# Graph network, layer 2: ScalarE fetches one more 128-row subtile of every four groups row by row

## The chip, the cores and the metric

The kernel runs on one core of a Trainium2 chip. The metric is the device time of one execution in microseconds (us). The core has five engines that work side by side, each with its own instruction stream: PE (matrix multiplications), DVE (elementwise work on tensors), ACT (ScalarE, one function per element), POOL (GpSimd; here it only issues gathers) and SP (SyncE; here it only issues transfers). An engine waits for another by a semaphore that the other counts up.

## The reference

Two message-passing layers run over one graph of 6250 nodes and 200000 edges. Both begin with a normalisation of the node features and a ReLU, and each adds its result to `x`. Layer 1 is an attention over the edges that end at a node. Layer 2, the one that the change touches, maps the node features, reads the row of each edge's source node, weighs it by a small network over the edge's features, and sums over the edges of each target node:

```python
s = s @ W_up_s * inv
v = jnp.einsum('nui,uw->nwi', v, W_up_v) * inv
h = jax.nn.silu(edge_feats @ A1 + b1)
h = jax.nn.silu(h @ A2 + b2)
w0, w1, w2, w3 = jnp.split(h @ A3, 4, axis=1)
ss, vs = s[sender], v[sender]
y_s, y_v = edge_attrs[:, :1], edge_attrs[:, 1:4]
out_s0 = ss * y_s * w0
out_s3 = jnp.einsum('eui,ei->eu', vs, y_v) / R3 * w3
out_v1 = ss[:, :, None] * y_v[:, None, :] * w1[:, :, None]
out_v2 = vs * y_s[:, :, None] * w2[:, :, None]
mji = jnp.concatenate([out_s0, out_s3, out_v1.reshape(E, 3 * MUL), out_v2.reshape(E, 3 * MUL)], axis=1)
message = jax.ops.segment_sum(mji, receiver, num_segments=num_nodes) / 10.0
```

The summed messages of a node are mapped once more by `W_out_s` and `W_out_v`.

## The kernel before

The edges are sorted by target. They are cut into tiles of 1024 edges, a tile into 8 subtiles of 128 (one edge per partition), and four tiles make a group. The place of a tile in its group is its slot s, 0 to 3. There are 49 groups; the code runs them in pairs by `groups` (L307), 24 turns of a loop with an even (e = 0) and an odd group (e = 1), and then one short group alone.

In layer 2 the engines share the work of a tile as follows.

- POOL gathers the source rows of 128 edges with one indirect transfer out of the table `up_tab` (L485), so 8 gathers for a tile. Before the gathers of a tile it waits until PE has summed the tile three places back, whose buffer it fills.
- SP spares POOL one gather in every two groups. The eighth subtile of slot 3 of the odd group is fetched by `fetch_single` (L396 to L402): 128 transfers of one row each, 80 of them during the even group and 48 during the odd one, in lots of 16 with one load of 16 row numbers into registers (L398). They land in one column of the row buffer, `single`. Per group SP then stores the finished node block (L438), loads the edge features (L415) once PE has used the old ones, and loads the edge attributes `y` (L411) once DVE has made the last message of the group (`msg1` of slot 3). All this stands in one queue, so the rows of the next group begin after that last wait.
- ACT runs the two Silu functions of the network for the tile two places ahead (`hidden`, L628 and L630). In slot 2 it also takes part in finishing a node block (`stage_block`): three copies, L635, L638 and L641, with two matrix products of PE between them (`map_block`, L1368 and L1372).
- PE makes, tile by tile and in this order: the radial weights of the next tile (L1358), the first product of the network for the tile two ahead (L1348), the sums of the first half tile (L1401), the second product of the network (L1352), the sums of the second half tile.
- DVE makes the messages of a tile in two halves of four subtiles, L1155 to L1167 each. The first of these instructions waits for the gathered rows. Then come the one-hot matrix of the next tile (L1086), the first weighing of the next tile (L1099), in slot 3 a copy of `y` (L1183), and the addition of the sums of the tile before (L1107). In slot 2 DVE ends with `add_block` (L1080), which adds the finished node block to `x` and waits for ACT's last copy.

No order is planned: each engine runs through its own code in the order written, and the semaphores set the rest.

Of the kernel before, what the change touches and what calls it, by code (L numbers as in the profile page):

```python
# [6 lines left out]
I32 = mybir.dt.int32  # L7
U8 = mybir.dt.uint8
BF16 = mybir.dt.bfloat16
ALU = mybir.AluOpType  # L10
# [32 lines left out]
FIRST = 80  # L43
ERP = 6 * HEADS
# [11 lines left out]
assert 0 < LT < HT and GI % 2 == 1 and QUADS <= 64 and AHEAD == 2 and U == 4  # L56
# [11 lines left out]
def gnn_kernel(nc, x, src, src_single, dst, dst_lin, edge_y, edge_f, bias, front, weights, out):  # L68

    with ExitStack() as ctx:  # L70
# [68 lines left out]
        early = sb("early", [P, max(NG * T, GI // 2 * P)])  # L139
        dst_rel = early[:, 0:NG * T].rearrange("p (g t) -> p g t", t=T)  # L140
        single_i = early[0:1, 0:GI // 2 * P].bitcast(I32)
        win_f = sb("win_f", [P, NG])
# [19 lines left out]
        w_aug = sb("w_aug", [P, LW])  # L162
        ones_row = sb("ones_row", [P, ZW])
        rows_all = sb("rows", [P, U * T + 1, ZW])
        rows = rows_all[:, 0:U * T, :].rearrange("p (u t) f -> p u t f", t=T)
        moved_on = rows_all[:, (U - 1) * T + 1:U * T + 1, :]
        single = rows_all[:, U * T, :]
# [30 lines left out]
        elr = part(3000, NB, 2 * HEADS)  # L198
        bound = part(3784, NB, HEADS)
# [72 lines left out]
        s_l2 = named("l2", ("h1", "h2", "tp", "first", "weighted", "dotted", "single")) | slot_sems("l2", ("h1_act", "h2_act")) \  # L272
# [41 lines left out]
        ROWS_IN = {"rows0": [GI * 16 * HT] * (U - 1) + [(GI - 1) * 16 * HT + 16 * LT],  # L314
                   "rows1": [GI * 16 * HT] * (U - 1) + [(GI - 1) * 16 * HT - GI // 2 * 16]}
# [3 lines left out]
        def slot_rows(s, fetched):  # L319

            return moved_on if fetched and s == U - 1 else rows[:, s, :, :]
# [22 lines left out]
        def _(sp):  # L344
# [61 lines left out]
            sp.dma_start(single_i, src_single).then_inc(loads["single"], 16)  # L406
# [67 lines left out]
        @block.gpsimd  # L474
        def _(pool):

            pool.memset(w_aug[:], 0.0).then_inc(zeroed, 1)
            pool.memset(ones_row[:], 0.0).then_inc(zeroed, 1)
# [4 lines left out]
            def gather(to, indices, table, width, done, n=T):  # L483
                for t in range(n):
                    pool.indirect_dma_start(out=to[:, t, 0:width], out_offset=None, in_=table,  # L485
                                            in_offset=bass.IndirectOffsetOnAxis(ap=indices[:, t:t + 1], axis=0))\
                        .then_inc(done[t // HT], 16)

            pool.wait_ge(G["flags_ready"], 1)
            general = pool.value_load(flags_i[0:1, 1:2], min_val=0, max_val=1)  # L490
            passes1 = pool.value_load(flags_i[0:1, 2:3], min_val=1, max_val=PASSES1)

            pool.wait_ge(s_in["stored_early"], 16 * REUSED)
            pool.wait_ge(s_in["stored"], 16 * (BI - REUSED))
            with pool.If(general > 0):
                with pool.Fori(0, NG) as g:
                    hold(pool, s_max["idx"], g + 1)
                    gather(rows[:, 0, :, :], idx_max, z_tab, ZW, (s_max["rows"],) * 2)
                hold(pool, s_max["free"], NG + 1)

            def gather_edges(tab, width, before, rows_stored):
                with pool.Fori(0, passes1) as k:
                    done = before + k
                    pool.sem_inc(s_l1["open"], 1)
                    if rows_stored:
                        pool.wait_ge(s_mid["stored"], rows_stored)

                    def four_tiles(q, r, e):
                        n = pool.snap(done * GI + q + 1, min_val=1, max_val=2 * PASSES1 * GI)
                        hold(pool, idx_set, done * SETS + q + 1)  # L510
                        for s in range(U):
                            hold(pool, s_l1["agg"][(s - 3) % U], n)
                            short, fetched = isinstance(r, int) and s == U - 1, e == 1 and s == U - 1
                            gather(slot_rows(s, fetched), idx[:, e, s, :], tab, width,
                                   (s_l1["rows0"][s], s_l1["rows1"][s]), LT if short else T - 1 if fetched else T)

                    groups(pool, four_tiles)
                    for half in ("rows0", "rows1"):
                        for s in range(U):
                            hold(pool, s_l1[half][s], ROWS_IN[half][s])  # L520
                    hold(pool, s_l1["msg1"][U - 1], (done + 1) * GI)
                    for half in ("rows0", "rows1"):
                        pool.inc_swdge_sem(s_l1[half], ROWS_IN[half], mode="sub")

            gather_edges(z_tab, ZW, 0, 0)
            gather_edges(up_tab, HIDDEN, passes1, 16 * NB)


        @block.scalar
        def _(act):  # L530
# [59 lines left out]

            with act.Fori(0, passes1) as k:
# [50 lines left out]

            last_stage = last_from(act)
            with act.Fori(0, passes1) as k:
# [7 lines left out]
                def four_tiles(q, r, e):  # L652
# [15 lines left out]
                groups(act, four_tiles)  # L668
# [9 lines left out]
        def _(dve):  # L678
# [85 lines left out]
            def node_rows(s, width):  # L764

                for first, last in ((0, SLOTS), (SLOTS, BI)):
                    if first > 0:
                        dve.wait_ge(s["stored_early"], 16 * REUSED)
                    with dve.Fori(first, last) as q:
# [4 lines left out]
                        for b in range(3):  # L774
# [4 lines left out]
                            if s is s_in:  # L779
                                v.tensor_copy(elr[:, bass.ds(q * BU + 3 * b, m), :], lin[:, :, MW:LW])  # L780
                                ins = v.tensor_tensor(to, lin[:, :, 0:width], bc(ones_row[:, :], 1, m), ALU.add)
# [212 lines left out]
            with dve.Fori(0, passes1) as k:  # L994
# [8 lines left out]
                def four_tiles(q, r, e):  # L1003
# [12 lines left out]
                    for s in range(U):  # L1016
                        h = s % 2
                        ts = slice(0, LT if last and s == U - 1 else T)
                        rows_s = slot_rows(s, e == 1)
                        el_e = rows_s[:, ts, MW:ZW]  # L1020

                        if last and s == U - 1:
                            dve.wait_ge(s_l1["rows0"][s], ROWS_IN["rows0"][s])
# [86 lines left out]
            with dve.Fori(0, passes1) as k:  # L1110
# [8 lines left out]
                def four_tiles(q, r, e):  # L1119
# [5 lines left out]
                    if not isinstance(r, int):  # L1125
                        landed_3 = dve.snap(landed_beside(r, e), min_val=16, max_val=GI * 16 * HT)
# [8 lines left out]
                    for s in range(U):  # L1135
                        h = s % 2
                        short = isinstance(r, int) and s == U - 1
                        for hf in range(1 if short else 2):
                            half = "rows0" if hf == 0 else "rows1"
                            dve.wait_ge(s_l1[half][s], ROWS_IN[half][s] if short else  # L1140
                                        landed_3 if s == U - 1 and hf == 1 else landed)
                            if e == 1 and s == U - 1 and hf == 1:
                                dve.wait_ge(s_l2["single"], fetched)
                            rows_s = slot_rows(s, e == 1)
# [48 lines left out]
                groups(dve, four_tiles)  # L1193
# [13 lines left out]
        def _(pe):  # L1207
# [27 lines left out]
            node_lin(s_in, w_aug[:, :], LW)  # L1235
# [10 lines left out]
            with pe.If(general > 0):  # L1246
                with pe.Fori(0, NG) as g:
                    pe.wait_ge(s_max["rows"], g * (16 * T) + 16 * T)
                    pe.wait_ge(s_max["free"], g + 1)
                    for i in range(T):  # L1250
                        mm = t.transpose(bank[i // 4][0:HEADS, (i % 4) * P:(i % 4) * P + P],
                                         rows[:, 0, i, MW:ZW], ident[:, :])
# [261 lines left out]
```

## Time and profile before

| | us |
|---|---|
| median of 3 runs | 3960.19 (3960.07 to 3960.31) |
| profiled execution | 3959.96 |
| its span in the trace | 3958.1 |
| PE, DVE, POOL busy in the span | 2594.4, 2490.1, 2913.5 |
| ACT busy in the span | 1006.3 |

The profiled execution lies within the runs. Layer 2 fills the time from 2020 us to the end. Register work, branches and the issue of transfers by SP and ACT are not counted as busy, so a busy share says little about SP, and on ACT it tells nothing of time spent on issuing.

### The profile page before, as it was taken

The page shows a single profiled execution, that of the slowest core. Times are in us where ns is not written, and L with a number is a line of the kernel's source. Part 1 is how long each engine was busy: PE and PEld are TensorE (multiplying, and loading weights), DVE is VectorE, ACT ScalarE, POOL GpSimd, SP SyncE. Part 2 cuts the span into 40 slices and gives each one's busy share as a digit, 9 for nine tenths or more (in the row PEclk, how much of TensorE's full clock was granted, in tenths as well). Part 3 has the DMA queues.
Part 4 walks back from the last instruction along what each step waited for, and adds up shares of the span by engine and source line. Part 5 has one row for each costly group of instructions (what it writes and reads, how often), then busy time and mean ns, then how long its engine had stood idle before and what let it go on. Part 6 is the DMA issues. An engine that isn't in the chain of part 4 may idle for free.

```text
span 3958.1 us, 64895 instructions
## 1 busy us (share of the span) xinstructions
PE 2594.4 (66%) x11162; PEld 1893.4 (48%) x11163; DVE 2490.1 (63%) x6074; ACT 1006.3 (25%) x1440; POOL 2913.5 (74%) x3088
## 2 busy tenths in 40 slices
PE   3545455545555555555578878787888888888887
PEld 2444444444444444444445555555555555555554
DVE  7444444444444444444467878887888878887787
ACT  4333333333333333333331111111111111111111
POOL 2777777777777777777767777777777777777776
PEclk8666666666666666666679999999999999999999
DMA  4222222222222222222212222222222222222221
GB/s 130 63 63 62 63 62 62 62 62 62 62 62 62 62 63 63 62 61 63 62 50 59 62 59 62 59 62 59 62 61 60 59 62 62 59 59 63 61 60 53
DMA packets 150584, 248.11 MB, mean 63 GB/s; under 512 B 59341, under 2 KB 97335, under 8 KB 150167
## 3 DMA queue, kind: packets, MB, share of 16 engines
q0 software_dynamic: 98496, 214.52, 21.8%
q1 hardware_dynamic: 51642, 30.27, 2.9%
q14 instruction: 297, 2.43, 0.2%
q10 hardware_dynamic: 144, 0.80, 0.1%
q8 instruction: 5, 0.08, 0.0%
HBM read 235.33 MB, written 10.03 MB: 62 GB/s over the span
## 4 chain that ended last, share of the span: by engine, by line
POOL 43%; issue 21%; PE 12%; DVE 8%; DMA 7%; SPq 5%; DVEq 1%; ACT 0%; POOLq 0%; ACTq 0%
POOL rows L485 43%; PE pair L1401 5%; PE pair L1322 5%; SPq L402 4%; DMA rows<-up_tab,idx 4%; DMA rows<-z_tab,idx 3%; DVE share L1044 2%; SPq L398 1%; PE pair L1358 1%; DVE share L1162 1%; DVE share L1158 1%; DVE acc L935 1%; PE pair L1348 1%; DVE share L1156 0%; PE pair L1352 0%
## 5 line engine op out<-in xcount | busy, mean ns | idle before, releaser
L485 POOL DMA_INDIRECT rows<-z_tab,idx x1539 | 1459.9, 949 | 539.9 <-issue 513.4
L485 POOL DMA_INDIRECT rows<-up_tab,idx x1539 | 1452.1, 944 | 487.3 <-issue 445.6
L1322 PE MATMUL pair<-share,acc 128*128 128x136 f32 x3126 | 750.3, 431 | 806.2 <-DVE share L1044 806.2
L1322 PEld LDWEIGHTS pair<-share,acc 128*128 128x128 f32 x3126 | 695.7, 324 | 939.9 <-DVE share L1044 937.9
L1401 PE MATMUL pair<-share,acc 128*128 128x256 f32 x3126 | 795.8, 399 | 295.2 <-DVE share L1167 291.7
L1401 PEld LDWEIGHTS pair<-share,acc 128*128 128x128 f32 x3126 | 574.9, 193 | 664.8 <-DVE share L1167 567.0
L1033 DVE TENSOR_TENSOR share<-rows,share 128x64 f32<-128x64 f32 x196 | 44.4, 226 | 855.6 <-DMA rows<-z_tab,idx 824.3
L1358 PE MATMUL pair<-weights_sb,share 128*128 128x256 f32 x1568 | 390.8, 394 | 30.5 <-ACT acc L641 29.1
L1155 DVE TENSOR_TENSOR share<-rows,pair 128x384 f32<-128x384 f32 x391 | 216.3, 553 | 302.2 <-DMA rows<-up_tab,idx 282.5
L628 ACT ACTIVATE share<-pair,front_sb 128x512 f32<-128x512 f32 x196 | 134.6, 687 | 927.0 <-PE pair L1348 927.0
L1358 PEld LDWEIGHTS pair<-weights_sb,share 128*128 128x128 f32 x1568 | 307.7, 199 | 84.1 <-issue 39.5
L606 ACT ACTIVATE pair<-share 128x64 f32<-128x64 f32 x196 | 44.6, 228 | 1073.0 <-DVE share L1038 1071.6
L630 ACT ACTIVATE share<-pair,front_sb 128x512 f32<-128x512 f32 x196 | 134.7, 687 | 489.4 <-PE pair L1352 487.3
L1044 DVE SCALAR_TENSOR_TENSOR share<-pair,rows 128x1088 f32<-128x1088 f32 x196 | 250.7, 1279 | 0.3 <-ACT pair L606 0.3
L935 DVE TENSOR_TENSOR acc<-acc,pair 128x1024 f32<-128x1024 f32 x196 | 239.1, 1220 | 0.1
L1086 DVE TENSOR_TENSOR acc<-acc,pair 128x1024 f32<-128x1024 f32 x196 | 237.5, 1212 | 0.0
L1162 DVE TENSOR_REDUCE share<-share 128x128 f32<-128x384 f32 x391 | 228.4, 584 | 0.0
L584 ACT ACTIVATE acc<-acc,ones 128x1024 bf16<-128x1024 bf16 x196 | 225.0, 1148 | 6.4
L1348 PE MATMUL pair<-ef_sb,weights_sb 64*128 64x512 f32 x392 | 223.4, 650 | 0.8 <-ACT share L630 0.8
L581 ACT ACTIVATE acc<-pair,acc 128x1024 bf16<-128x1024 f32 x196 | 215.8, 1101 | 25.2 <-PE pair L1265 25.2
L1158 DVE TENSOR_TENSOR share<-rows,pair 128x384 f32<-128x384 f32 x391 | 213.6, 546 | 0.0
L1164 DVE TENSOR_TENSOR share<-share,pair 128x384 f32<-128x384 f32 x391 | 212.1, 542 | 0.0
(168 smaller groups left out, 2384.8 us busy)
## 6 DMA issues: line engine op xcount, KB each, us to landing
rows<-z_tab SPq DMA_DIRECT2D x3072, 0.6 KB
rows<-up_tab SPq DMA_DIRECT2D x3072, 0.5 KB
rows<-z_tab,idx POOLq DMA_INDIRECT x1539
rows<-up_tab,idx POOLq DMA_INDIRECT x1539
ef_sb<-in_edge_f SPq DMA_DIRECT2D x50, 128.0 KB
z_tab<-rows SPq DMA_DIRECT2D x7, 504.0 KB, 3.2
y_sb<-in_edge_y SPq DMA_DIRECT2D x50, 64.0 KB
x_sb<-in_x SPq DMA_DIRECT2D x7, 448.0 KB, 7.0
```

What stands on the lines that cost most here:

```text
L485: pool.indirect_dma_start(out=to[:, t, 0:width], out_offset=None, in_=table, in_offset=bass.IndirectOffsetOnAxis(ap=indices[:, t:t + 1], a ...
L584: nc.scalar.activation(to, to, ACT.Relu, bias=ones[:, 0:1], scale=-2.0).then_inc(s_l1["turned"][s], 1)
L935: v.tensor_tensor(hot[:, s, :, :], bc(dst_col[:, bass.ds(group, 1), :].rearrange("p a t -> p (a t)"), 2, P), bc(iota_l1, 1, T), ALU.is_equal)
L1044: v.scalar_tensor_tensor(out=msg[:, h, ts, :].rearrange("p t (h f) -> p t h f", f=RW), in0=bc(a_ps[h][:, ts, :], 3, RW), scalar=1.0, in1=r ...
L1086: v.tensor_tensor(hot[:, s, :, :], bc(dst_col[:, bass.ds(group, 1), :].rearrange("p a t -> p (a t)"), 2, P), bc(iota_l2, 1, T), ALU.is_equal)
L1155: v.tensor_tensor(vy, vecs, y_v, ALU.mult)
L1158: v.tensor_tensor(cell[:, :, 0:96].rearrange("p t (i u) -> p t i u", u=MUL), vecs, bc(w[:, :, 2 * MUL:3 * MUL], 2, 3), ALU.mult)
L1162: v.tensor_reduce(dots, vy.rearrange("p t i u -> p t u i"), AX.X, ALU.add)\
L1322: mm = t.matmul(bank[2 + h][:, 0:MW], hot[:, s, i, :], msg[:, h, i, :], start=(i == 0), stop=(i == tiles - 1))
L1348: t.matmul(bank[4], a1_bd[at, s, :], ef_sb[at, :], start=True, stop=True).then_inc(s_l2["h1"], 1)
L1358: mm = t.matmul(bank[2 * (s % 2) + j // 2][:, (j % 2) * 256:(j % 2) * 256 + 256], h2_sb[:, s % 2, j * P:(j + 1) * P], a3_bd[:, :], start=T ...
L1401: mm = t.matmul(bank[6 + s % 2][:, 0:MSG], hot[:, s, j, :], msg2[:, s % 2, hf, j % HT, :], start=(j == 0), stop=(j == tiles - 1))
```

## The change

In layer 2, POOL no longer gathers the first subtile of slot 2 in every fourth group (f = 3, with f the place of a group in a loop over four groups). ACT fetches its 128 rows by one-row transfers into a new column of the row buffer, `ahead`. It does so in 13 lots of 12 and 8 rows, one behind the second Silu of each tile from slot 0 of f = 0 to slot 0 of f = 3. In slot 2 the lot stands ahead of ACT's work on the node block. DVE waits for the rows ahead of the first half of that tile, and ACT waits in slot 3 of f = 3 until DVE has used them. The layer-2 loops of POOL, ACT and DVE are now four groups long (`groups4`); those of SP and PE keep their length. Layer 1 keeps its gathers. To make room, two small tensors (`w_aug`, `ones_row`) move into a shared buffer.

```diff
+STEPS = (12, 8) * 6 + (8,)
...
+        rows_all = sb("rows", [P, U * T + 2, ZW])
+        ahead = rows_all[:, 2 * T, :]
+        single = rows_all[:, U * T + 1, :]
...
+        def groups4(eng, body):
+
+            with eng.Fori(0, GI // 4) as w:
+                for f in range(4):
+                    body(w * 4 + f, w * 2 + f // 2, f % 2, w, f)
+            body(GI - 1, GI // 2, 0, GI // 4, 0)
...
-            gather_edges(z_tab, ZW, 0, 0)
-            gather_edges(up_tab, HIDDEN, passes1, 16 * NB)
+                            in_front = f == 3 and s == 2
+                            gather(slot_rows(s, beside or in_front), idx[:, e, s, :], tab, width,
+                                   (s_l1["rows0"][s], s_l1["rows1"][s]), 1 if in_front else 0,
+                                   LT if short else T - 1 if beside else T)
...
+            gather_edges(z_tab, ZW, 0, 0, ROWS0["z"], groups)
+            gather_edges(up_tab, HIDDEN, passes1, 16 * NB, ROWS0["up"], groups4)
...
+            def fetch_ahead(tab, width, w, step, fetched):
+
+                first = sum(STEPS[:step])
+                _, nodes = nc.values_load_multi_w_load_instructions(
+                    ahead_i[0:1, bass.ds(w * P + first, STEPS[step])], engines=(mybir.EngineType.Activation,), min_val=0,
+                    max_val=NODES - 1, skip_runtime_bounds_check_because="they are sources, below NODES")
+                for i, node in enumerate(nodes):
+                    act.dma_start(ahead[first + i:first + i + 1, 0:width], tab[bass.ds(node, 1), 0:width])\
+                       .then_inc(fetched, 16)
...
+                        if not isinstance(r, int) and f * U + s < len(STEPS):
+                            fetch_ahead(up_tab, HIDDEN, w, f * U + s, s_l2["ahead"])
+                        if f == 3 and s == 3:
+                            hold(act, s_l1["msg0"][2], n_2)
                         if s == 2:
                             hold(act, s_l1["added"][0], n)
                             blocks(act, mybir.EngineType.Activation, q + 1, stage_block)
...
-                groups(act, four_tiles)
+                groups4(act, four_tiles)
...
+                            if in_front and hf == 0:
+                                dve.wait_ge(s_l2["ahead"], fetched_2)
...
-                groups(dve, four_tiles)
+                groups4(dve, four_tiles)
```

On POOL, the loop of layer 2 before: two groups to a turn, 32 and 31 gathers (L307 is the loop, L284 a wait).

```order
L307 ISA
L284 ISA
L485 DMA rows<-up_tab,idx 128x128 x32
L284 ISA x2
L485 DMA rows<-up_tab,idx 128x128 x31
L307 REGISTER_ALU
L307 COMPARE_AND_BRANCH
```

The same loop on POOL in the change, where the lines are L316, L286 and L502:

```order
L316 ISA
L286 ISA
L502 DMA rows<-up_tab,idx 128x128 x32
L286 ISA x2
L502 DMA rows<-up_tab,idx 128x128 x31
L286 ISA x2
L502 DMA rows<-up_tab,idx 128x128 x32
L286 ISA x2
L502 DMA rows<-up_tab,idx 128x128 x30
L316 REGISTER_ALU
L316 COMPARE_AND_BRANCH
```

Four groups took two turns with 126 gathers; they now take one with 125.

On ACT, slot 2 of a group before, from the first Silu to the first copy of the node block (L284 is the wait for DVE's addition, L289 and L290 load the numbers of the blocks that are ready):

```order
L627 REGISTER_ALU
L628 ACTIVATE share<-pair,front_sb 128x512
L630 ACTIVATE share<-pair,front_sb 128x512
L284 ISA
L289 TENSOR_LOAD ready
L289 ISA x2
L290 ISA
L290 TENSOR_LOAD ready
L290 ISA x2
L291 COMPARE_AND_BRANCH
L292 UNCONDITIONAL_BRANCH
L292 ISA
```

The same place on ACT in the change, at f = 0 (the Silu lines are L657 and L659, the wait is L286; the pair of L617 rows stands there 12 times, once a row fetched):

```order
L657 ACTIVATE share<-pair,front_sb 128x512
L659 ACTIVATE share<-pair,front_sb 128x512
L613 ISA
L613 TENSOR_LOAD early
L617 ISA
L617 DMA rows<-up_tab 1x128
...
L286 ISA
L291 ISA
L291 TENSOR_LOAD ready
L291 ISA x2
L292 ISA
```

The load of the 12 row numbers and the 12 transfers stand between the second Silu and everything that ACT does for the node block. Counted in the same listing, one turn of the loop of layer 2 has 256 rows on DVE and 67 on ACT before, and 514 and 414 now.

## Rows read from the trace of the kernel before

**Rows 1.** Stretch: length, busy of PE, PEld, DVE, ACT, POOL, granted clock, DMA share, GB/s.

```profile
2100.00:3000.00 900.00, 728.89 (x2696) 485.74 (x2696) 722.83 (x1786) 152.48 (x271) 680.17 (x721) 0.99 0.23 60
```

**Rows 2.** POOL's groups of instructions, 2100 to 3900 us: busy, mean ns, idle before.

```profile
L485 POOL DMA_INDIRECT rows<-up_tab,idx x1442 | 1360.6, 944 | 439.9 <-issue 399.9 <-PE pair L1401 39.9
```

**Rows 3.** Waits of DVE, 2100 to 3900 us: total, times, longest.

```profile
DVE share L1155 <- DMA rows<-up_tab,idx: 268.2, 154, 2.3
DVE x_sb L1080 <- ACT acc L641: 64.5, 43, 2.8
DVE share L1155 <- DMA rows<-up_tab: 5.6, 4, 2.3
```

**Rows 4.** Timeline of DVE: one tile without a wait, start and duration.

```profile
2264.78 0.55 DVE L1155 TENSOR_TENSOR share<-rows,pair 128x384 f32<-128x384 f32 x1
2272.56 0.55 DVE L1155 TENSOR_TENSOR share<-rows,pair 128x384 f32<-128x384 f32 x1
```

**Rows 5.** Timelines of DVE and then ACT: slots 2 and 3 of one group.

```profile
2401.26 0.56 DVE L1155 TENSOR_TENSOR share<-rows,pair 128x384 f32<-128x384 f32 x1
2412.53 0.55 DVE L1155 TENSOR_TENSOR share<-rows,pair 128x384 f32<-128x384 f32 x1
2417.32 0.28 DVE L1167 TENSOR_TENSOR share<-share,pair 128x128 f32<-128x128 f32 x1
2420.49 0.55 DVE L1155 TENSOR_TENSOR share<-rows,pair 128x384 f32<-128x384 f32 x1
...
2406.78 0.69 ACT L630 ACTIVATE share<-pair,front_sb 128x512 f32<-128x512 f32 x1 [2.74 <-PE pair L1352]
2408.34 0.42 ACT L635 ACTIVATE acc<-acc 128x256 f32 x1 [0.87 <-issue]
2410.67 0.38 ACT L638 ACTIVATE acc<-pair 128x256 f32<-128x256 f32 x1 [1.91 <-PE pair L1368]
2411.85 0.28 ACT L641 ACTIVATE acc<-pair 128x128 f32<-128x128 f32 x1 [0.80 <-PE pair L1372]
2415.61 0.69 ACT L628 ACTIVATE share<-pair,front_sb 128x512 f32<-128x512 f32 x1 [3.48 <-PE pair L1348]
```

**Rows 6.** Timeline of PE: the transposes for the node block of that group.

```profile
2410.25 0.38 PE L1368 MATMUL pair<-front_sb,acc 128*128 128x128 f32 x2
```

**Rows 7.** Timeline of SP's transfers: one turn of its loop.

```profile
2658.99 39.44 SPq L402 DMA_DIRECT2D rows<-up_tab  x80
...
2702.36 0.37 SPq L411 DMA_DIRECT2D y_sb<-in_edge_y  x1
2704.02 23.11 SPq L402 DMA_DIRECT2D rows<-up_tab  x48
...
2732.26 0.36 SPq L411 DMA_DIRECT2D y_sb<-in_edge_y  x1
2737.55 2.43 SPq L402 DMA_DIRECT2D rows<-up_tab  x6
```

**Rows 8.** SP's loads of `y` at both ends of another turn, and DVE within it.

```profile
3600.02 0.36 SPq L411 DMA_DIRECT2D y_sb<-in_edge_y  x1
...
3677.35 0.36 SPq L411 DMA_DIRECT2D y_sb<-in_edge_y  x1
...
3674.51 0.56 DVE L1155 TENSOR_TENSOR share<-rows,pair 128x384 f32<-128x384 f32 x1 [2.26 <-DMA rows<-up_tab]
```

**Rows 9.** The page's queue of fetched instructions: packets, MB, share of 16 engines.

```profile
q14 instruction: 297, 2.43, 0.2%
```

**Rows 10.** SP's one-row transfers of layer 2: min, median, max ns.

```profile
L402 SPq DMA_DIRECT2D rows<-up_tab x3072: 237/237/320, 2020.1 to 3909.2; - x192
```

**Rows 11.** Timelines of ACT and SP at the start.

```profile
0.73 0.40 ACTq L543 DMA_DIRECT2D share<-in_dst  x1
...
0.74 0.40 SPq L345 DMA_DIRECT2D front_sb<-in_front  x1
```

**Rows 12.** A stretch behind a pause of PE, columns as in rows 1.

```profile
2217.60:2221.00 3.40, 3.01 (x7) 2.48 (x8) 3.29 (x10) 0.00 (x0) 2.49 (x3) 0.50 0.23 61
```

More of the change, by code:

```diff
@@ L54 @@
 LW = ZW + HEADS
-assert 0 < LT < HT and GI % 2 == 1 and QUADS <= 64 and AHEAD == 2 and U == 4
+assert 0 < LT < HT and GI % 4 == 1 and sum(STEPS) == P and QUADS <= 64 and AHEAD == 2 and U == 4
 assert NB == BU * BI and NG == U * GI and NG * GE >= EDGES and PAD_DST >= NODES + 3 * P and WIN + HALF - 1 <= P
@@ L271, in gnn_kernel @@
                                                          "exp", "msg0", "msg1", "agg", "added", "rows0", "rows1"))
-        s_l2 = named("l2", ("h1", "h2", "tp", "first", "weighted", "dotted", "single")) | slot_sems("l2", ("h1_act", "h2_act")) \
+        s_l2 = named("l2", ("h1", "h2", "tp", "first", "weighted", "dotted", "single", "ahead")) | slot_sems("l2", ("h1_act", "h2_act")) \
             | {n: sems(f"l2_{n}_buf", 2) for n in ("y", "ef")}
@@ L405, in _ @@
             sp.wait_ge(G["columns_set"], 1)
-            sp.dma_start(single_i, src_single).then_inc(loads["single"], 16)
+            sp.dma_start(singles_i, src_single).then_inc(loads["single"], 16)
             sp.wait_ge(s_in["stored_early"], 16 * REUSED)
@@ L481, in _, with gather @@
             pool.memset(minus_id, 0.0).then_inc(zeroed, 1)
-            def gather(to, indices, table, width, done, n=T):
-                for t in range(n):
+            def gather(to, indices, table, width, done, first=0, last=T):
+                for t in range(first, last):
                     pool.indirect_dma_start(out=to[:, t, 0:width], out_offset=None, in_=table,
@@ L497, in _, with gather_edges @@
                     hold(pool, s_max["idx"], g + 1)
-                    gather(rows[:, 0, :, :], idx_max, z_tab, ZW, (s_max["rows"],) * 2)
+                    gather(slot_rows(0), idx_max, z_tab, ZW, (s_max["rows"],) * 2)
                 hold(pool, s_max["free"], NG + 1)
-            def gather_edges(tab, width, before, rows_stored):
+            def gather_edges(tab, width, before, rows_stored, landed0, over):
                 with pool.Fori(0, passes1) as k:
@@ L512, in four_tiles @@
                             hold(pool, s_l1["agg"][(s - 3) % U], n)
[L513 to L518, printed above, removed]
+                            short, beside = isinstance(r, int) and s == U - 1, e == 1 and s == U - 1
+                            in_front = f == 3 and s == 2
+                            gather(slot_rows(s, beside or in_front), idx[:, e, s, :], tab, width,
+                                   (s_l1["rows0"][s], s_l1["rows1"][s]), 1 if in_front else 0,
+                                   LT if short else T - 1 if beside else T)
+                    over(pool, four_tiles)
+                    for half, rows_in in (("rows0", landed0), ("rows1", ROWS1)):
                         for s in range(U):
-                            hold(pool, s_l1[half][s], ROWS_IN[half][s])
+                            hold(pool, s_l1[half][s], rows_in[s])
                     hold(pool, s_l1["msg1"][U - 1], (done + 1) * GI)
-                    for half in ("rows0", "rows1"):
-                        pool.inc_swdge_sem(s_l1[half], ROWS_IN[half], mode="sub")
-            gather_edges(z_tab, ZW, 0, 0)
-            gather_edges(up_tab, HIDDEN, passes1, 16 * NB)
+                    for half, rows_in in (("rows0", landed0), ("rows1", ROWS1)):
+                        pool.inc_swdge_sem(s_l1[half], rows_in, mode="sub")
+            gather_edges(z_tab, ZW, 0, 0, ROWS0["z"], groups)
+            gather_edges(up_tab, HIDDEN, passes1, 16 * NB, ROWS0["up"], groups4)
         @block.scalar
@@ L641, in stage_block @@
                 nc.scalar.activation(moved, mapped_ps, ACT.Copy).then_inc(s_out["moved"], 1)
+            act.wait_ge(loads["single"], 16)
             last_stage = last_from(act)
```

65 lines of the change are left out of this document (40 added, 25 removed).

## The prediction

> **What bounds the kernel now.** I read four views, in this order. First the windows: in layer 2 no engine is busy all the time; in 900 us POOL works 680 us, PE 729, DVE 723 [rows 1]. So I asked who waits. POOL's gathers take 944 ns each, and the idle time in front of them, 439.9 us over 1442 gathers, is mostly put down to "issue", a wait for nothing that the profile shows [rows 2]. One gather therefore costs (1360.6 + 439.9) / 1442 = 1.249 us, back to back. DVE waits 154 times, 268.2 us in all, for POOL's rows, and only 4 times for SP's [rows 3]. POOL sets the pace: two groups have 63 gathers, 63 x 1.249 = 78.7 us, and SP's loop repeats after 2737.55 - 2658.99 = 78.56 us [rows 7].
>
> Two other chains are close behind, and the reader should see how close. DVE needs 2272.56 - 2264.78 = 7.78 us for a tile without a wait [rows 4], 7.96 for slot 3 and 11.27 for slot 2 of this group, which finishes a node block [rows 5] (a wait for late rows lies inside it, but ACT's work on the block ends later anyway). SP's loop is the other. In one turn DVE stood 2.26 us for SP's rows, and SP's load of `y` came 3677.35 - 3600.02 = 77.33 us after that of the turn before [rows 8]. That is what SP needs when nobody delays it: 1.2 us less than POOL.
>
> **What is removed.** Twelve gathers: 12 x 1.249 = 15.0 us, if POOL stays the bound. Four groups then take 125 x 1.249 = 156.1 us instead of 157.3 (measured 2 x 78.56 = 157.1). The other chains must fit into 156.1.
>
> **What is added on ACT.** 128 one-row transfers per four groups. The nearest rows are SP's, with the same instructions: 80 rows take 39.44 us and 48 take 23.11, so (39.44 - 23.11) / 32 = 0.510 us a row, loads of the row numbers included [rows 7]. A lot of 12 costs 6.1 us, one of 8 costs 4.1. The ends: the transfer instruction alone takes 0.237 us [rows 10], so 2.8 us for 12; above 0.510 I have no row, only two queues in each other's way (below). I take 0.510, since it is the same sequence.
>
> In slots 0, 1 and 3 the lot lies beside other work. The second Silu starts 5.52 us into the tile [rows 5], the lot of 12 ends at 11.6, and the next first Silu would be due at 7.78 + 3.08 = 10.9 (3.08 is 2415.61 - 2412.53). It comes 0.7 us late, but the second Silu sat idle 2.74 us before it started [rows 5], which takes that up. Without this cover, each lot of 12 would cost 0.7 us.
>
> In slot 2 nothing covers it when the group finishes a block. Behind the lot on ACT stand the wait for DVE's addition, the loads of the block numbers and the three copies; PE waits for these copies, and DVE waits at L1080 for the last. From DVE's first instruction of slot 2 to that of slot 3 [rows 5]: 5.52 to the second Silu; 6.1 for the lot; 1.56 from that Silu to the first copy; 0.84 to the second copy (0.42 for the first copy, and 0.42 from PE's transposes at 2410.25 [rows 6] to the second copy; today's 2.33 holds a wait for PE's sums, which will be over by then); 1.18 to the third; 0.68 to slot 3. The sum is 15.9 us, against 11.27 today. About every group finishes one block: 43 waits at L1080 in 45 groups [rows 3]. Groups without one give time back and those with two cost more; I let these cancel, plus or minus 10 us on the total.
>
> **What is added at the loop's end.** At a turn of SP's loop, the first row follows the load of `y` after 5.29 us (2737.55 - 2732.26); within a turn the same step takes 1.66 (2704.02 - 2702.36) [rows 7]. So SP pays 3.63 us for a jump back. The queue of fetched instructions moved 297 packets, 2.43 MB [rows 9], so some loop is fetched again at every turn. DVE passes the end of a pair without a wait: 3.17 us from its last message instruction to the next group's first [rows 5], all of it work. Its loop doubles from 256 to 514 listed rows, longer than SP's. The price of the new turn lies between 0, as DVE pays now, and 3.63, as SP pays. I take 2.0, a little above the middle: DVE's engine still has some 3 us of work behind its last message, and how far its instruction stream is ahead of that no row shows. ACT's loop grows as well; its stall lies beside DVE's.
>
> The Trainium skill, "Runtime: NRT & Kernel Launch", section "Instruction fetch mechanics", speaks against the change here: it says that an engine holds 512 instructions in two pages, and that a jump out of them waits for a fetch. The trace agrees that a jump can cost 3.63 us on SP. By this rule DVE would pay the whole of it, and the sum below would be 12 x 1.63 = 20 us higher, about 3992.
>
> **The sum.** Take SP's turns, which end with the last message of an odd group. From the end of f = 3 to that of f = 1, DVE runs back to back: 2.89 to the next group (2420.49 - 2417.60), 2.0 for the jump, 15.56 for two tiles, 15.9, 7.96, 15.56, 15.9, and 5.07 to the last message of slot 3 (2417.60 - 2412.53): 80.8 us. SP cannot begin the rows of f = 2 before that, since its rows stand behind the wait for this message. From there to the end of f = 3, DVE needs 2.89 + 15.56 + 15.9 + 7.96 + 15.56 + 11.27 + 5.07 = 74.2, but SP needs 77.3, and its rows end the wait. Four groups take 80.8 + 77.3 = 158.1 us, against 157.1 before and 156.1 for POOL. That is 1.0 us more in each of 12 turns: 12 us on the profiled execution's 3959.96 (the median of the runs is 0.2 higher), so **3972 us**, 0.3% slower. The gain from POOL is given back twice over: DVE and ACT lose it in the slots with a block, and SP, which can't run ahead of DVE, can't make it up.
>
> Three edits I cost at nothing. DVE's wait for the rows of `ahead`: the last lot is in slot 0 of f = 3, two tiles (15.6 us) ahead; if it were late, its remainder would be paid. ACT's wait in slot 3 of f = 3 for DVE's use of them: DVE has passed that a tile earlier, and behind it stands only the set of indices, which waits for a later message anyway. PE's clock: behind a pause PE was granted 0.50, the lower level of 1.2 GHz, for 3.4 us with 3.01 busy [rows 12], and the lot makes PE pause some 6 us. At full clock this work would take 1.5 us less; DVE needs PE's next weights only at the end of its two halves, some 5 us on, so I count 0; without that cover it is up to 1.5 in each of the two slots, 36 us in all.
>
> **The rivals.** *The gain is kept, POOL stays the bound: 3959.96 - 15.0 = 3945.* It decides once the chain is 2.0 us shorter than my 158.1. One thing suffices: no stall at DVE's jump, or 0.425 instead of 0.510 us a row in the two lots of 12 that are in the way (24 x 0.085 = 2.0). For it: DVE shows no stall at a turn now, and the transfer itself takes 0.237 us. Against it: SP pays both prices in full. Chance 0.30.
>
> *Half of each: no change.* With a stall of 0.5 to 1.5, or rows of 0.45 to 0.49 us, four groups take 156.6 to 157.8, so 3953 to 3968. The rows are fetched by another engine and nothing comes of it. Chance 0.16.
>
> *ACT's and SP's transfers get in each other's way.* During ACT's lots SP issues as many rows. If a row waits while the other engine's 0.237 us [rows 10] run, it finds them with a chance of 0.237 / 0.510 and waits half of them: 0.055 us. For the 48 rows in the half of the turn that SP bounds this is 2.6 us, 12 x 2.6 = 32; the two lots of 12 add 24 x 0.055 = 1.3, another 16: 4004 to 4020. Against it: at the start ACT and SP issued at 0.73 and 0.74 us and both took 0.40 [rows 11], side by side. Chance 0.10. The Trainium skill, "Perfetto Trace Analysis", section "DMA Instruction — HWDGE (DVE, Sync)", has the generator of descriptors locked for exclusive use, which would be this rival; the two rows at the start do not bear it out.
>
> **How the numbers follow.** My forecast has 0.44, with a range of its own of 3962 to 3992 (the blocks' 10 us below, the whole stall above). Of that, 0.10 is for the full stall of 3.63 us at each jump, 3992 (12 x 1.63 = 20 us more). The range for 8 in 10 reaches down to the gain kept, 3943, and up to 4000; it leaves out the contention and a clock that costs its full price. A measurement of this kernel can tell about 0.2%, 8 us, from no change. Faster by more than that: the first rival and a little, 0.31. Within it: the second and the low edge of the forecast, 0.20. Slower: 0.49.
>
> **What would show it.** Right: POOL waits for PE's sums (L1401) by more than 0.3 us, at least from the middle of layer 2, instead of never; the wait at L1080 grows from 1.5 to about 6 us in groups f = 0, 1, 2; a gap of about 2 us at DVE's jump; and in f = 3, DVE waits for SP's rows. Wrong: POOL's gathers still follow each other at 1.249 us to the end (then the chain fits and 3945 holds), ACT's rows under 0.43 us, no gap at the jump, or one-row transfers of more than 0.237 us on SP while ACT fetches.

## The result and the profile after

The changed kernel takes 4037.89 us (median of 4 runs, 4035.47 to 4039.77), against 3960.19 before: a ratio of 1.0196 (95% interval 1.0178 to 1.0214), 78 us slower where 12 were forecast. The time lies outside the range. The profiled execution took 4035.47 us, with a span of 4033.6.

The lost time is all in layer 2. The waits of DVE and of POOL in the changed kernel, from 2100 to 3900 us (total, times, longest), answer to [rows 2, 3]:

```profile
DVE x_sb L1115 <- ACT acc L670: 344.7, 42, 13.1
DVE share L1199 <- issue: 22.6, 11, 2.4
DVE share L1199 <- DMA rows<-up_tab: 20.7, 11, 4.6
DVE share L1199 <- DMA rows<-up_tab,idx: 1.9, 2, 1.3
...
L502 POOL DMA_INDIRECT rows<-up_tab,idx x1378 | 1301.6, 945 | 498.9 <-issue 407.9 <-PE pair L1445 91.0
POOL rows L502 <- PE pair L1445: 91.0, 45, 9.3
```

DVE no longer waits for POOL's rows (1.9 us for 268.2). It waits for ACT's last copy of the node block instead, 8.2 us each time for 1.5 (344.7 / 42; 64.5 / 43 before). POOL waits for PE's sums by up to 9.3 us: the bound has moved from POOL to the chain through DVE, ACT and PE. The same stretch by engine, to be read beside [rows 1], has the granted clock of TensorE as its third number from the end:

```profile
2100.00:3000.00 900.00, 746.10 (x2600) 508.37 (x2601) 690.34 (x1721) 149.12 (x264) 653.34 (x692) 0.88 0.23 59
```

PE finished fewer products in it (2600 for 2696) and was busy longer, at 0.88 of full clock for 0.99. Slot 2 of the group at f = 1 shows where that comes from: the timelines of DVE, ACT and PE, and two stretches of it with the clock.

```profile
3064.56 0.55 DVE L1199 TENSOR_TENSOR share<-rows,pair 128x384 f32<-128x384 f32 x1
3083.20 0.29 DVE L1115 TENSOR_TENSOR x_sb<-x_sb,acc 128x128 f32 x1 [10.92 <-ACT acc L670]
3083.47 0.56 DVE L1199 TENSOR_TENSOR share<-rows,pair 128x384 f32<-128x384 f32 x1
...
3062.62 0.69 ACT L657 ACTIVATE share<-pair,front_sb 128x512 f32<-128x512 f32 x1 [5.42 <-issue]
3065.50 3.27 ACTq L617 DMA_DIRECT2D rows<-up_tab  x8
3071.82 0.69 ACT L659 ACTIVATE share<-pair,front_sb 128x512 f32<-128x512 f32 x1 [2.10 <-PE pair L1396]
3073.02 5.07 ACTq L617 DMA_DIRECT2D rows<-up_tab  x12
3079.89 0.42 ACT L664 ACTIVATE acc<-acc 128x256 f32 x1 [7.38 <-issue]
3081.08 0.38 ACT L667 ACTIVATE acc<-pair 128x256 f32<-128x256 f32 x1 [0.78 <-PE pair L1412]
3082.78 0.28 ACT L670 ACTIVATE acc<-pair 128x128 f32<-128x128 f32 x1 [1.31 <-PE pair L1416]
...
3080.36 0.69 PE L1412 MATMUL pair<-front_sb,acc 128*128 128x128 f32 x2 [6.85 <-ACT acc L664]
3083.46 3.65 PE L1402 MATMUL pair<-weights_sb,share 128*128 128x256 f32 x8 [0.72 <-ACT acc L670]
...
3071.00:3079.00 8.00, 2.50 (x10) 1.52 (x8) 1.26 (x4) 0.69 (x1) 6.17 (x7) 0.85 0.23 60
3079.00:3083.50 4.50, 1.95 (x7) 1.27 (x7) 0.30 (x2) 1.08 (x3) 3.28 (x5) 0.50 0.34 88
```

From DVE's first instruction of slot 2 to that of slot 3 it takes 18.91 us (15.9 were forecast). Term by term, forecast in brackets: 7.26 to the second Silu (5.52), 8.07 from there to the first copy (7.66), 1.19 to the second (0.84), 1.70 to the third (1.18), 0.69 to slot 3 (0.68). The lot itself costs 0.4 us more than was said. But PE, which waits 6.85 us for the first copy, comes back at 0.50 of its clock, the 1.2 GHz level. Its transposes take 0.69 us for 0.38 [rows 6], and the weights for the next tile 3.65 us, where 1.89 is their duration at full clock elsewhere in this trace. Over the groups that finish one block (the first turn left out), slot 2 takes 17.6, 19.3 and 18.8 us on average at f = 0, 1 and 2, and the clock is 0.50 from the first copy to slot 3 in every one of them.

SP's loads of `y` at the ends of the two halves of that turn:

```profile
3003.59 0.36 SPq L428 DMA_DIRECT2D y_sb<-in_edge_y  x1
...
3088.79 0.36 SPq L428 DMA_DIRECT2D y_sb<-in_edge_y  x1
...
3166.36 0.36 SPq L428 DMA_DIRECT2D y_sb<-in_edge_y  x1
```

The first half takes 85.2 us (80.8 forecast), the second 77.6 (77.3). The shape of the sum was right; the error sits in the first half, which holds two of the three blocks with a lot ahead of them; most of what the third loses is hidden behind SP.

### The profile page after: what moved, and what is told of

It is laid out like the page before. It is cut to its first block, busy times and chain, and to the rows that moved or that the text cites. A ratio compares the mean times of both kernels' runs of the same rounds, so it can differ in the third digit from the quotient of the medians.

```text
span 4033.6 us, 69793 instructions
## 1 busy us (share of the span) xinstructions
PE 2674.5 (66%) x11162; PEld 1967.3 (49%) x11163; DVE 2477.2 (61%) x6074; ACT 1009.8 (25%) x1440; POOL 2904.6 (72%) x3076
## 4 chain that ended last, share of the span: by engine, by line
POOL 25%; PE 22%; issue 20%; SPq 12%; DVE 10%; ACTq 6%; DMA 3%; ACT 1%; DVEq 1%; POOLq 0%
POOL rows L502 25%; SPq L419 9%; PE pair L1445 7%; PE pair L1366 4%; PE pair L1402 4%; ACTq L617 4%; DMA rows<-z_tab,idx 3%; PE pair L1392 2%; PE pair L1396 2%; SPq L415 2%; DVE share L1079 2%; PE pair L1416 1%; DVE share L1206 1%; ACTq L613 1%; DVE share L1202 1%
## 5 line engine op out<-in xcount | busy, mean ns | idle before, releaser
L502 POOL DMA_INDIRECT rows<-up_tab,idx x1527 | 1442.3, 945 | 571.2 <-issue 469.2
L502 POOL DMA_INDIRECT rows<-z_tab,idx x1539 | 1460.8, 949 | 539.6 <-issue 513.3
L1366 PEld LDWEIGHTS pair<-share,acc 128*128 128x128 f32 x3126 | 696.1, 324 | 940.5 <-DVE share L1079 938.5
L1445 PEld LDWEIGHTS pair<-share,acc 128*128 128x128 f32 x3126 | 597.3, 196 | 370.7 <-issue 197.1
L1402 PE MATMUL pair<-weights_sb,share 128*128 128x256 f32 x1568 | 445.3, 435 | 30.5 <-ACT acc L670 29.0
L1402 PEld LDWEIGHTS pair<-weights_sb,share 128*128 128x128 f32 x1568 | 340.1, 220 | 97.4 <-issue 42.7
L657 ACT ACTIVATE share<-pair,front_sb 128x512 f32<-128x512 f32 x196 | 134.7, 687 | 753.2 <-PE pair L1392 534.4
L1115 DVE TENSOR_TENSOR x_sb<-x_sb,acc 128x128 f32 x49 | 14.6, 297 | 396.2 <-ACT acc L670 374.9
L1199 DVE TENSOR_TENSOR share<-rows,pair 128x384 f32<-128x384 f32 x391 | 215.8, 552 | 68.3 <-issue 25.3
L659 ACT ACTIVATE share<-pair,front_sb 128x512 f32<-128x512 f32 x196 | 134.7, 687 | 428.8 <-PE pair L1396 428.8
L1392 PE MATMUL pair<-ef_sb,weights_sb 64*128 64x512 f32 x392 | 238.7, 691 | 0.8 <-ACT share L659 0.8
L1396 PE MATMUL pair<-share,weights_sb 128*128 128x512 f32 x392 | 209.1, 616 | 20.2 <-ACT share L657 20.2
```

The lines of the kernel that those rows point to most:

```text
L1366: mm = t.matmul(bank[2 + h][:, 0:MW], hot[:, s, i, :], msg[:, h, i, :], start=(i == 0), stop=(i == tiles - 1))
L1392: t.matmul(bank[4], a1_bd[at, s, :], ef_sb[at, :], start=True, stop=True).then_inc(s_l2["h1"], 1)
L1396: t.matmul(bank[4], a2_bd[:, :], h1_sb, start=True, stop=True).then_inc(s_l2["h2"], 1)
L1402: mm = t.matmul(bank[2 * (s % 2) + j // 2][:, (j % 2) * 256:(j % 2) * 256 + 256], h2_sb[:, s % 2, j * P:(j + 1) * P], a3_bd[:, :], start=T ...
L1445: mm = t.matmul(bank[6 + s % 2][:, 0:MSG], hot[:, s, j, :], msg2[:, s % 2, hf, j % HT, :], start=(j == 0), stop=(j == tiles - 1))
```

## The experiments

Theory A: the lot in front of the block in slot 2 is the loss, by its length and by what the pause does to PE's clock. Rival B: ACT's issuing delays the Silu functions in whatever slot it stands. Rival C: the loops of four groups are too long. Each ratio is to the kernel before on the same chip.

**The lot behind the block.**

```diff
-                        if not isinstance(r, int) and f * U + s < len(STEPS):
-                            fetch_ahead(up_tab, HIDDEN, w, f * U + s, s_l2["ahead"])
                         if f == 3 and s == 3:
                             hold(act, s_l1["msg0"][2], n_2)
                         if s == 2:
                             hold(act, s_l1["added"][0], n)
                             blocks(act, mybir.EngineType.Activation, q + 1, stage_block)
+                        if not isinstance(r, int) and f * U + s < len(STEPS):
+                            fetch_ahead(up_tab, HIDDEN, w, f * U + s, s_l2["ahead"])
```

> The change, with ACT's lot of slot 2 behind its work on the node block instead of ahead of it; the same 13 lots, the same loops. Theory A (the loss sits in slot 2: the lot stands in front of the block's three copies, and the pause that it gives PE lowers PE's clock, which makes the rest of the tile longer): slot 2 of a group with a block falls from 17.3 to 18.9 us back to about 11.5, POOL is the bound again, 3945 to 3952 us. Rival B (ACT's issuing delays the Silu functions wherever the lot stands, and PE and DVE with them): the lot still delays the first Silu of slot 3, over 4000 us. Rival C (the loops of four groups are too long, and their jumps and fetches cost the time): no change from 4038 us.

Measured: 3951.41 us, ratio 0.9963 (0.9949 to 0.9977), 14.5 us less than before. DVE's waits, 2100 to 3900 us:

```profile
DVE share L1199 <- DMA rows<-up_tab,idx: 232.3, 143, 3.0
DVE x_sb L1115 <- ACT acc L670: 66.5, 46, 3.0
DVE share L1199 <- issue: 22.6, 11, 2.3
```

DVE waits for POOL's rows again, and the block costs it 1.4 us a time as before the change. The same 128 rows, on the same engine, in the same loops, now cost nothing, and POOL's gain of 15.0 us arrives. Rivals B and C fall as explanations of the 78 us; B comes back below in a weaker form.

**The loops alone.** POOL gathers everything, ACT fetches nothing, the loops stay four groups long. The counts that POOL and DVE wait for follow, and ACT's wait in slot 3 of f = 3 goes (not shown).

```diff
-                            in_front = f == 3 and s == 2
+                            in_front = False
...
-                        if not isinstance(r, int) and f * U + s < len(STEPS):
-                            fetch_ahead(up_tab, HIDDEN, w, f * U + s, s_l2["ahead"])
```

> The loops of four groups on POOL, DVE and ACT alone: POOL gathers every subtile as before the change, ACT fetches nothing. Theory A: DVE shows a gap of 2.05 us at each of its 12 jumps, as in the changed kernel, but it lies inside the time that DVE waits for POOL's rows anyway: 3958 to 3963 us. Rival C: the 12 jumps and the fetches cost 25 us or more, 3985 us and up. Rival B has nothing to say: 3960 us.

Measured: 3965.44 us, ratio 1.0000 (0.9990 to 1.0009), with 3965.86 for the kernel before on this chip; it is the ratio that answers the expectation. DVE's waits:

```profile
DVE share L1195 <- DMA rows<-up_tab,idx: 252.2, 145, 2.3
DVE share L1195 <- issue: 21.5, 11, 2.1
```

The jump is there, 21.5 / 11 = 1.95 us each, but DVE would have waited for POOL anyway. Rival C is out.

**PE kept busy through the pause.** The clock alone: the lots stay, and PE runs products that nobody reads before it waits for ACT. PE's loop becomes four groups long for it.

```diff
+            def keep_busy():
+                for _ in range(24):
+                    t.matmul(bank[0][:, 0:MSG], ident[:, :], a3_bd[:, :], start=True, stop=True)
...
+                            if f < 3 and not isinstance(r, int):
+                                keep_busy()
                             blocks(pe, mybir.EngineType.PE, q + 1, map_block)
...
-                groups(pe, four_tiles)
+                groups4(pe, four_tiles)
```

> The change, and in addition PE runs 24 products whose result nobody reads, in slot 2 of the groups f = 0, 1, 2, between its sums and its wait for ACT's first copy, where it stood idle for about 7 us (PE's loop is made four groups long for it). It prices the clock alone: the lots stay where they are. Theory A with the clock as a part of it: PE's stages in the block go from 1.19 and 1.69 us (between ACT's copies) to 0.95 and 1.18, the Silu functions come in time again, slot 2 takes 16.3 to 16.6 us in all three groups, and the time is 3985 to 4005 us. If the clock has no part: slot 2 stays at 17.3 to 18.9, 4030 to 4040 us.

Measured: 4078.27 us, ratio 1.0285 (1.0268 to 1.0303). Outside both expectations, and inconclusive: the 24 products took 10.52 us, longer than the pause, and delayed the block themselves. So the same with 14:

> As the run with PE kept busy, with 14 products for 24: the 24 took 10.5 us, 3.2 us longer than the pause that they were to fill, and 14 take 6.1. It prices the clock alone. If the lower clock has a part in the loss: slot 2 with a block takes 16.3 to 16.6 us in f = 0, 1 and 2 (5.52 to the second Silu, 8.2, 0.94, 1.19, 0.68), and the ratio to the kernel before is 1.004 to 1.012. If not: 1.018 to 1.021, as the change.

Measured: 3996.83 us, ratio 1.0091 (1.0074 to 1.0108). Slot 2 of one group at f = 1, DVE and then ACT:

```profile
2412.39 0.55 DVE L1199 TENSOR_TENSOR share<-rows,pair 128x384 f32<-128x384 f32 x1
2428.81 0.56 DVE L1199 TENSOR_TENSOR share<-rows,pair 128x384 f32<-128x384 f32 x1
...
2417.91 0.69 ACT L659 ACTIVATE share<-pair,front_sb 128x512 f32<-128x512 f32 x1 [2.36 <-PE pair L1396]
2425.99 0.42 ACT L664 ACTIVATE acc<-acc 128x256 f32 x1 [7.39 <-issue]
2426.93 0.38 ACT L667 ACTIVATE acc<-pair 128x256 f32<-128x256 f32 x1 [0.53 <-PE pair L1416]
2428.12 0.28 ACT L670 ACTIVATE acc<-pair 128x128 f32<-128x128 f32 x1 [0.80 <-PE pair L1420]
```

16.42 us: 5.52, 8.08, 0.94, 1.19, 0.69. The clock is kept: 0.95 to 1.00 from the first copy to slot 3 in all groups with one block at f = 0, 1 and 2 (the first turn left out), and PE's steps there are short in each. The second Silu comes earlier at f = 1 and 2, after 6.03 and 6.10 us on average for 7.59 and 7.48 in the change, but later at f = 0, after 6.67 for 5.76. So slot 2 kept to the expected 16.6 us in 10 of these 28 groups only; in the others it took 17.0 to 18.8. PE's longer loop is no rival for the gain: PE waits put down to "issue" are 1.4 us in the change and 2.7 here, from 2100 to 3900 us. The work added to PE made the kernel (1.0196 - 1.0091) x 3960 = 42 us faster than the change. That is the clock's part of the 78, less what the products themselves cost, and 36 us remain.

**No rows in slot 2, and what went wrong with that.**

```diff
-STEPS = (12, 8) * 6 + (8,)
+STEPS = (14, 14, 0, 14) * 3 + (2,)
```

> The change with no rows in slot 2: lots of 14 in slots 0, 1 and 3, and 2 in the last one. Theory A2 (the lot in front of the block delays DVE; only when DVE is late and must run at 7.8 us a tile do the lots of the other slots delay the Silu functions too, since at POOL's pace of 9.8 us they fit): slot 2 takes 11.5 us, POOL stays the bound, ratio 0.995 to 0.998. Rival B (a long lot delays the Silu functions in any slot, whatever the pace): the lots of 14 are the longest of all, ratio above 1.01.

Measured: 4023.89 us, ratio 1.0167 (1.0150 to 1.0184), a miss for theory A2. The loads of the row numbers on ACT (L613), minimum, median and maximum in ns, show why: for this kernel, then for one with lots of 12, 12, 0 and 16 rows (below).

```profile
L613 ACTq TENSOR_LOAD <-early x120: 669/1414/3244, 2041.3 to 3949.6; - x120
...
L613 ACTq TENSOR_LOAD <-early x120: 730/967/1068, 2040.7 to 3869.5; - x120
```

Some loads take over 3 us, although they fetch 14 numbers at most. They are those of the lots that begin at row 14, 42, 70 and 98, two past a multiple of four; the lots of 14 from 0, 28, 56, 84 and 112 took 1.2 to 1.4. To test it, each load starts at the multiple of four below and drops the first two numbers; rows, slots and lots are the same.

```diff
-                    ahead_i[0:1, bass.ds(w * P + first, STEPS[step])], ...
+                    ahead_i[0:1, bass.ds(w * P + (first - first % 4), STEPS[step] + first % 4)], ...
-                for i, node in enumerate(nodes):
+                for i, node in enumerate(nodes[first % 4:]):
```

> The run with lots of 14 and none in slot 2, where a load of row numbers that started two past a multiple of four took 3.1 to 3.2 us and one that started at a multiple of four 1.2 to 1.4. Now each load starts at the multiple of four below (16 numbers, of which the first two are not used); rows, places and lots are the same. If the start of the load is the cause: those loads take 1.1 to 1.5 us, and with 2 us less in every second lot the ratio falls from 1.017 to 0.996 to 1.003. If rather 14 rows are too many for the slots (rival B): the loads may be shorter, but the ratio stays over 1.01.

Measured: 3952.59 us, ratio 0.9970 (0.9959 to 0.9982). The loads:

```profile
L613 ACTq TENSOR_LOAD <-early x120: 495/1226/1441, 2043.3 to 3881.1; - x120
```

That settles the miss. It also says what is left of rival B: lots that are some 2 us longer, in slots 0, 1 and 3, do cost time, since they delay the second Silu of slot 2 and the block behind it. With the slow loads it came 11.6 to 14.8 us into slot 2 (means at f = 0 to 2, groups with one block), where the kernel before has 5.7 to 5.8. With the padded ones it is still late, 8.4 to 11.1 us, but this stays hidden: four groups take 156.6 us on average, POOL's pace.

**Four rows, ahead of the block and behind it.** Both have lots of 14, 10, 4 and 10 rows, so both have such slow loads too.

```diff
+STEPS = (14, 10, 4, 10) * 3 + (14,)
```

> The change with lots of 14, 10, 4 and 10 rows in slots 0 to 3 (and 14 in the last one), so slot 2 has 4 rows ahead of the block instead of 12 and the other slots have more. Theory A: the lot of 4 takes about 2.1 us, slot 2 with a block takes some 13.6 us, DVE's group 37 us, under POOL's 39: 3945 to 3955 us. Rival B: the lots of 14 delay the Silu functions more than those of 12, over 4040 us. Rival C: 4038 us.

Measured ahead of the block: 4085.3 us, ratio 1.0321 (1.0261 to 1.0380). That is far above what theory A expected, and is what rival B said.

> The lots of 14, 10, 4 and 10 rows that gave 1.032, with the 4 rows of slot 2 behind the block instead of ahead of it; nothing else differs. Theory A2: those 2.1 us ahead of the block were what set DVE behind POOL, and with them gone everything fits again: 0.995 to 0.998. Rival B: the lots of 14 and 10 were the loss, 1.02 to 1.03.

Measured behind it: 3953.96 us, ratio 0.9986 (0.9976 to 0.9995). This is a little above what theory A2 expected, and rival B is out: the lots and the slow loads (2.2 to 2.5 us for 10 numbers, 3.2 to 3.4 for 14) are the same in both, and the second Silu of slot 2 is late in both, 7.7 to 12.7 us ahead of the block and 8.1 to 10.7 behind it (means at f = 0 to 2). The place of four rows alone is worth 3.3% here. Without the slow loads the same four rows ahead of the block give 1.0031 (next), so the slow loads and these four rows cost far more together (3.2%) than either alone (nothing, and 0.3%).

**The number of rows ahead of the block.** 128 rows in all, every lot at a multiple of four. Slot 2 has 0, 4, 8, 12 (the change) or 16 rows, and the other slots share the rest.

```diff
+STEPS = (12, 12, 0, 16) * 3 + (8,)
...
+STEPS = (12, 12, 4, 12) * 3 + (8,)
...
+STEPS = (8, 12) * 6 + (8,)
...
+STEPS = (8, 8, 16, 8) * 3 + (8,)
```

> No rows in slot 2, lots of 12, 12 and 16 in slots 0, 1 and 3 and 8 in the last: every lot starts at a multiple of four rows, so that no load of row numbers takes 3.2 us, as half of those did in the run with lots of 14. Theory A2 (the lot in front of the block is the loss): ratio 0.995 to 0.999. Rival B (as many rows on ACT cost the same in any slot): 1.015 to 1.02, as with the lots of 14.

> 4 rows in slot 2 ahead of the block, 12 in the three other slots, 8 in the last lot, all from multiples of four rows. Theory A2: the lot ahead of the block takes 2.2 us, slot 2 some 14 us, and DVE's group of 37 to 38 us is still under POOL's 39; with 8 rows the ratio was 1.010 and with 12 it was 1.020, so by that line 0.997 to 1.003. Rival B: about 1.02, since the rows are as many.

> The change with the two sizes swapped: 8 rows in slots 0 and 2, 12 in slots 1 and 3; the lot of slot 2 is still ahead of the block. Theory A2: the lot of 8 takes 4.0 us for 5.5, so slot 2 takes some 15.8 us in f = 0, and DVE still falls behind POOL: ratio 1.005 to 1.015. Rival B: as many rows in all, 1.02. If the lot's place in slot 2 did not matter in proportion to its length: 1.02 as well.

> 16 rows in slot 2 ahead of the block, 8 in all other slots. Theory A2: 1.6 us more ahead of each block than in the change, ratio 1.025 to 1.035. Rival B: the other slots have less, so 1.01 to 1.02.

| rows in slot 2 | median us | ratio to before | 95% interval |
|---|---|---|---|
| 0 | 3945.02 | 0.9961 | 0.9947 to 0.9975 |
| 4 | 3971.97 | 1.0031 | 1.0015 to 1.0048 |
| 8 | 4000.89 | 1.0103 | 1.0086 to 1.0119 |
| 12 | 4037.89 | 1.0196 | 1.0178 to 1.0214 |
| 16 | 4083.24 | 1.0316 | 1.0299 to 1.0333 |

The loss grows with the rows in front of the block, by 0.7% to 1.2% for each four. ACT fetches 128 rows in all five, so the sum of its rows does not explain it, and the other slots have most rows where the loss is least. The stages behind the ratios were longer than theory A2 expected: slot 2 with one block took 14.7, 16.1 and 17.2 us on average at f = 0, 1 and 2 with four rows (some 14 expected), and 16.9 at f = 0 with eight (15.8). With four rows theory A2 expected that DVE would still keep under POOL's pace (0.997 to 1.003); 1.0031 lies just outside, and its ten runs spread from 3957.78 to 3983.88, which fits a point where DVE's chain and POOL are nearly even. In the kernel with none, slot 2 of a group runs nearly as before the change:

```profile
3022.80 0.55 DVE L1199 TENSOR_TENSOR share<-rows,pair 128x384 f32<-128x384 f32 x1
3033.95 0.29 DVE L1115 TENSOR_TENSOR x_sb<-x_sb,acc 128x128 f32 x1 [1.25 <-ACT acc L670]
3034.21 0.55 DVE L1199 TENSOR_TENSOR share<-rows,pair 128x384 f32<-128x384 f32 x1
```

11.41 us, with 11.27 in [rows 5]. At 3945.02 us it is 15.3 us faster than the kernel before on the same chip (3960.29): the whole price of twelve gathers. It is the best version found; the one with the lot behind the block is as good within the intervals.

## Why the prediction was wrong

**Right in its mechanism.** Twelve gathers are worth 15.0 us (15.3 and 14.5 measured, where nothing else was in the way). The lot stands on DVE's path in slot 2, POOL ends up waiting for PE's sums, and DVE waits at its last block instruction, as forecast. The rival in which the gain is kept was worked out to the right time, 3945, but not to the right condition: it takes the lot out of the way of the block.

**The step that failed: "PE's clock ... so I count 0".** The forecast saw that the lot would make PE pause, and priced the lower clock at up to 36 us, but took it for covered: DVE needs PE's next weights only some 5 us on. That looked at one product. The lower clock lies also on the path of the block (1.19 and 1.70 us for 0.94 and 1.18 between ACT's copies) and behind it on PE, whose next products feed the Silu functions that ACT needs before the next lots. The run with 14 products sets the clock's part at 42 us. That this is close to the 36 is luck: the 36 were counted for another path, the weights that DVE waits for.

**The second term that was too small: the second Silu at 5.52 us.** I took the Silu functions as in time in slots 0 and 1, 0.7 us late at worst and covered. In the changed kernel the second Silu of slot 2 came after 5.76 us on average at f = 0, but after 7.59 and 7.48 at f = 1 and 2, and after 7.26 in the group shown. PE's rows ahead of that group, and one of its waits from 2100 to 3900 us, say why:

```profile
3041.00 3.77 PE L1402 MATMUL pair<-weights_sb,share 128*128 128x256 f32 x8 [0.72 <-ACT acc L670]
3044.70 1.70 PE L1392 MATMUL pair<-ef_sb,weights_sb 64*128 64x512 f32 x2
...
3063.36 1.12 PE L1396 MATMUL pair<-share,weights_sb 128*128 128x512 f32 x2 [0.46 <-ACT share L657]
...
PE pair L1396 <- ACT share L657: 15.2, 25, 2.5
```

Behind the block of f = 0, at the lower clock, the weights and the first product take 3.77 and 1.70 us; at full clock they take 1.89 and 1.12. So PE is 2.46 us late. From there to the next block it waits once, 0.46 us, for a first Silu that the lot of 12 in slot 0 held back (the row at 3062.62, idle 5.42, "issue"), and it has not caught up by the second Silu of f = 1. The lots' hold on the first Silu cost PE at most 15.2 us in all of that stretch. The two errors are thus largely one: the clock makes PE late, and PE makes the Silu late. The cover was counted at POOL's pace of some 9.8 us a tile; a DVE that is late runs its tiles at 7.78 [rows 4], and then PE and ACT have too little slack beside it to catch up.

Of the 36 us that remain without the clock's part, 12 were forecast. For the other 24 there is an estimate from the run with 14 products: at f = 0 and 1, slot 2 with one block took 17.73 and 16.93 us on average for 15.9, 2.9 more in the two together. Of these, 1.7 are a second Silu that is still late (6.67 and 6.03 for 5.52) and 1.0 are the way from there to the first copy (8.25 and 8.08 for 7.66). No run separates the two.

**Sized right.** A lot of 12 on ACT: 8.07 us from the second Silu to the first copy, with 7.66 forecast. The jump of DVE's loop: 22.6 / 11 = 2.05 us each, with 2.0 forecast; since that was a choice between 0 and 3.63, it is in part luck. The page's queue of fetched instructions moved 435 packets for 297:

```profile
q14 instruction: 435, 3.56, 0.3%
```

The Trainium skill, "Runtime: NRT & Kernel Launch", section "Instruction fetch mechanics", by which DVE would pay for a jump, holds in kind: the gap appeared with the longer loop, though with 2.05 us and not SP's 3.63. That it costs time does not follow, since in the run with the loops alone it was covered. SP's bound in the second half: 77.6 us for 77.3.

**The contention rival.** It gave 4004 to 4020 and would have been the nearest, for a wrong reason. The one-row transfers of ACT and of SP in the changed kernel, minimum, median and maximum in ns:

```profile
L617 ACTq DMA_DIRECT2D rows<-up_tab x1536: 234/235/588, 2041.2 to 3973.4; - x192
L419 SPq DMA_DIRECT2D rows<-up_tab x3072: 237/237/321, 2019.2 to 3986.1; - x192
```

SP's median is that of [rows 10] to the nanosecond. The rival lets fewer than half of the rows wait, which a median need not show, but the mean does not move either: it is 241 ns in both traces, and in the changed kernel 242 for SP's 1022 rows that ran while one of ACT's did and 240 for the others; the rival had 55 ns more. The lock of the descriptor generator that the Trainium skill, "Perfetto Trace Analysis", section "DMA Instruction — HWDGE (DVE, Sync)", speaks of does not show between these two queues.

**The range.** It left out the contention and "a clock that costs its full price". It was the second of these that came.

## What to carry to other kernels

Work that is "free" on an idle engine is free only behind the last thing in its stage that another engine waits for: the same 128 rows gave back 15 us behind the block's copies or in other slots, and cost 78 with slot 2's lots ahead of them. In the other slots it is free only as far as the slack there goes: four loads in ten that were 2 us longer took the gain back. Before pricing a delay on one engine, ask which other engine it leaves idle and at what clock that one comes back; here a pause of some 7 us of PE was paid again in the products behind it. And a cover that is counted at the pace of the bound is gone once another chain has become the bound.

## What the runs showed of the hardware that had not been expected

A load of numbers into ACT's registers depends on where it starts. In the run with lots of 14 from a multiple of four the loads took 1.2 to 1.4 us, and from two past it 3.0 to 3.2; 16 numbers from the multiple of four below, in the place of the latter, took 1.0 to 1.2. These 16 are even faster than 14 from a multiple of four, so the end of a load seems to matter as well; no run tests that by itself. The start of these loads alone turned a kernel at 0.9970 into one at 1.0167.

Idle time of PE can be worth filling with products that nobody reads: 14 of them in each pause, 6 us of added work, made the changed kernel about 1% faster (1.0091 for 1.0196). It is no cure here, since moving the lot removes the pause.
